# A third block of the masked scores copied by ScalarE instead of multiplied by VectorE, in the feature stage of a four-stage network

## What is computed

```
q = softmax_features(x @ Wq @ Kq)     # softmax of f and of -f, joined: 128 features a head
k = softmax_features(x @ Wk @ Kk)
v = x @ Wv                            # 16 heads of 64
A = causal(q @ k.T)                   # 256 x 256 of a head: zero where the key is later than the query
y = (A @ v) / (sum of A over the keys + 1e-12)
out = y @ Wo
```

## Time and profile before

| | |
|---|---|
| runs of the kernel before | 4855.63 us median of 3 (4854.26 to 4864.38) |
| the profiled execution | 4866.69 us, its span 4865.1 us |
| the feature stage's heads | about 557 to 1280 us of the span |
| busy over 532 to 1280 us (748 us) | PE 706.80, weight loads 584.97, DVE 663.52, ACT 261.51, POOL 456.72 us |
| granted TensorE clock over the same | 0.98 |

### The profile page before, as it was taken

One profiled execution on the slowest core, in us unless ns is written; L12 is line 12 of the kernel. 1 busy time (PEld: TensorE's weight loads), 2 busy tenths in 40 slices (PEclk: granted clock), 3 DMA queues, 4 the chain that ended last, 5 costly groups with the idle time before them and its releaser, 6 DMA issues. The chain is left out here.

```text
span 4865.1 us, 172713 instructions
## 1 busy us (share of the span) xinstructions
PE 4276.7 (88%) x70208; PEld 3382.3 (70%) x70208; DVE 4016.8 (83%) x6281; ACT 3049.4 (63%) x5515; POOL 2776.0 (57%) x1392
## 2 busy tenths in 40 slices
PE   5797799999578999989999999899989999999995
PEld 4565487787557777777777777777777777777774
DVE  5334799999689998989888989989999899898983
ACT  3365333333156777777777777777777777777763
POOL 0222566666266666656666666666666666666661
PEclk9699799999789999999999999999999999999997
DMA  1233000000122324333333233332333323333232
GB/s 49 86 131 123 0 1 0 0 0 0 36 54 62 72 63 93 69 73 68 77 85 70 59 75 81 80 71 63 71 87 77 69 59 75 86 72 74 61 69 56
DMA packets 239188, 303.61 MB, mean 62 GB/s; under 512 B 93940, under 2 KB 129272, under 8 KB 237944
## 3 DMA queue, kind: packets, MB, share of 16 engines
q1 hardware_dynamic: 223192, 247.08, 22.3%
q0 software_dynamic: 15264, 46.14, 3.0%
HBM read 50.37 MB, written 28.84 MB: 16 GB/s over the span
## 5 line engine op out<-in xcount | busy, mean ns | idle before, releaser
L2094 POOL TENSOR_TENSOR raw<-raw,rs 128x1024 f32<-128x1024 f32 x384 | 792.0, 2063 | 985.3 <-DVE rs L1933 628.8
L2086 POOL TENSOR_TENSOR spare<-raw,table 128x1024 f32<-128x1024 f32 x384 | 914.3, 2391 | 261.9 <-DVE raw L1912 251.1
L1905 DVE TENSOR_TENSOR raw<-raw,table 128x1024 f32<-128x1024 f32 x384 | 772.1, 2011 | 55.0 <-POOL spare L2086 53.4
L1779 ACT ACTIVATE raw<-shared 128x512 f32<-128x512 f32 x768 | 463.3, 603 | 309.8 <-PE shared L1559 285.8
L1557 PE MATMUL shared<-wqkv_lo,xT_hi 128*128 128x512 f32 x1152 | 559.8, 486 | 38.9 <-DVE xT_lo L1942 30.1
L1899 DVE TENSOR_REDUCE ss<-spare 128x16 f32<-128x1024 f32 x384 | 466.3, 1215 | 135.2 <-ACT spare L1784 134.6
L1912 DVE TENSOR_TENSOR raw<-raw,spare 128x1024 f32<-128x1024 f32 x384 | 551.0, 1435 | 13.2
L1612 PE MATMUL trn<-ident,raw 128*128 128x128 f32 x3072 | 483.7, 280 | 15.8 <-POOL raw L2094 3.9
L1558 PE MATMUL shared<-wqkv_hi,xT_lo 128*128 128x512 f32 x1152 | 470.4, 408 | 0.0
L1559 PE MATMUL shared<-wqkv_hi,xT_hi 128*128 128x512 f32 x1152 | 469.9, 408 | 0.0
L1784 ACT ACTIVATE spare<-shared 128x512 f32<-128x512 f32 x768 | 462.2, 602 | 1.8 <-DVE ss L1899 1.8
(11 more groups left out here) (203 smaller groups left out, 9740.4 us busy)
## 6 DMA issues: line engine op xcount, KB each, us to landing
Vw<-V SPq DMA_DIRECT2D x1344, 128.0 KB
xs<-X SPq DMA_DIRECT2D x144, 128.0 KB, 2.4
Vw<-V SPq DMA_DIRECT2D x192, 64.0 KB
e_plain<-in_L_ffn_W SPq DMA_DIRECT2D x16, 704.0 KB, 4.7
split_hi<-e_high POOLq DMA_DIRECT2D x16, 704.0 KB, 5.9
split_lo<-e_low POOLq DMA_DIRECT2D x16, 704.0 KB, 7.0
wqkv_hi<-split_hi POOLq DMA_DIRECT2D x30, 256.0 KB, 3.2
wqkv_lo<-split_lo POOLq DMA_DIRECT2D x30, 256.0 KB, 3.3
```

What stands on the lines that cost most here:

```text
L1905: dve.tensor_tensor(x, x, table[:, part, 0, k][:, None, :].to_broadcast([P, H, HD]), ALU.mult).then_inc(cos_part, 1)
L2086: pool.tensor_tensor(dst, src, by[:, None].to_broadcast([P, H, 2, 32]), ALU.mult).then_inc(sin_part, 1)
L2094: pool.tensor_tensor(x, x, rs[:, at:at + H][:, :, None].to_broadcast([P, H, HD]), ALU.mult).then_inc(rotated, 1)
```

## The change

DVE's `mask` multiplies blocks 0 and 2 alone (a view of 2x128 columns with the 128 between them skipped, against one 128-column triangle read twice). ACT gets a new first instruction in every step, `cross(n, h)`, which copies the middle block of head h from PSUM to `at` unchanged. It waits for DVE's `masked` of the same head, so that the two engines don't read the tile at once, and for `mix(h-2)`. A new semaphore `crossed` counts the copies; `scores(h)` and `mix(h)` of PE wait for it beside `masked`.

```
@@ def scores(n, par, h, first):            # PE
                 if not (first and h < 2):
                     pe.wait_ge(masked, count(N - 1))
+                    pe.wait_ge(crossed, count(N - 1))
@@ def mix(n, par, h, first=False):         # PE
                 N = n * H + h
                 pe.wait_ge(masked, count(N + 1))
+                pe.wait_ge(crossed, count(N + 1))
@@ ACT
+            def cross(n, h, first):
+
+                N = n * H + h
+                act.wait_ge(masked, count(N + 1))
+                if not (first and h < 2):
+                    act.wait_ge(mixed, count(N - 1))
+                act.activation(at[:, h % 2, P:SEQ], sco[h % 2][:, P:SEQ], ACT.Copy).then_inc(crossed, 1)
@@ def heads(n, par, first=False, ahead=2): # ACT
                 for h in range(H):
+                    cross(n, h, first)
                     if ahead >= 1:
                         project(n + 1, 1 - par, h)
@@ def mask(n, h, first):                   # DVE
-                dve.tensor_tensor(at[:, h % 2], sco[h % 2][:, 0:3 * P], tri[:], ALU.mult).then_inc(masked, 1)
+                own, to = (x.rearrange("p (c t) -> p c t", t=P)[:, 0:3:2] for x in (sco[h % 2][:, 0:3 * P], at[:, h % 2]))
+                dve.tensor_tensor(to, own, tri[:, None, 0:P].to_broadcast([P, 2, P]), ALU.mult).then_inc(masked, 1)
```

More of the change, by code:

```diff
@@ L761, in feature_stage @@
         masked = sem("g_masked")
+        crossed = sem("g_crossed")
         mixed = sem("g_mixed")
```

## The result

The changed kernel takes 4902.09 us (median of 4 runs, 4898.67 to 4906.06) against 4856.03 for the kernel before on the same chip: ratio 1.0093, 95% interval [1.0079, 1.0106], 46 us slower. The forecast was 4877 with a range to 4894. The sign was right and the size less than half of what came. The profiled execution of the change took 4898.67 us, its span is 4897.1 us.

What follows compares the result with a forecast made beforehand. PE was taken to bound the feature stage, DVE close behind; 1.89 + 0.24 - 0.60 = 1.53 us a sequence over 14 sequences, 21.4 us, gave 4888, or 4877 with medians 11 us lower; range 4848 to 4894.

Steps and rivals of the forecast that it cites:

- What the copy holds up: On ACT, the copy waits for the mask and delays the projection's emptying, so PE waits 1.89 us more a sequence.
- Six places: Projections said to be held at heads 1, 2, 6, 9, 10 and 11, by 0.08 to 0.66 us each.
- The handoff that no row showed: From DVE's mask end to ACT's copy: between 0 and 0.2 us, taken as 0.10.
- The mix of head 13: PE's wait in step 14: the mix needs 0.79 us from its mask's start instead of 0.55, 0.24 more.
- The edge at head 12: ACT's exponential of 1.90 us holds the emptying, which starts 2.46 us after the last; 2.62 are there.
- So the whole wait of 0.60 goes: PE's wait for kept features ahead of step 0's scores vanishes: masks 13 to 15 sooner by 0.39, PE later by 0.24.
- PE's added waits cost nothing where they are met: PE's extra semaphore waits were given no cost, as no idle time showed ahead of turns with three semaphores.
- ACT's emptying isn't held up: Rival: the emptying is done before PE asks; only the two old waits change, -5 us, 4851; chance 0.20 including up to +10.
- DVE's saving in full: Rival: the copy hides, both old PE waits shrink and all 26.9 us go, 4829; chance 0.08, in full or large part.
- The wait on the mask is what carries this term: On ACT, a copy released by the scores alone would hold nothing up and leave the first rival's price, 4851.
- PE's wait for `gen` grows from 1.0 us to about 26: Sign in the changed profile: PE's wait for ACT's emptying of the projection buffer, in five or six places of a sequence.
- The period is about 47.9: Sign in the changed profile: a sequence of the feature stage takes about 47.9 us, where it took 46.40.

Runs made afterwards that it cites:

- copy_behind_drain: The changed kernel with ACT's copy moved behind the emptying of the projection buffer, ahead of the exponential: 4872.78 us, ratio 1.0035 to the kernel before.
- short_mask_no_copy: The kernel before with DVE's mask over blocks 0 and 2 only, the middle block set once to 1.0, no copy: 4856.68 us, ratio 1.0001.
- before_two_more_waits: The kernel before with one always met semaphore wait more on PE at each scores and each mix: 4868.45 us, ratio 1.0027.
- change_one_wait: The changed kernel with PE waiting for `crossed` alone at scores and mix, `masked` dropped: 4888.87 us, ratio 1.0064 to the kernel before.
- full_mask_and_copy: The changed kernel with DVE's mask over all three blocks again and ACT's copy kept: 4921.12 us, ratio 1.0125 to the kernel before.

## Why the prediction was right and wrong

- **What the copy holds up: right.** "So a mask that was needed by the mix, late in step h+1, is now needed before the projection, early in it" is what copy_behind_drain undid. Six places were named, all six came, and no other; 1.89 us a sequence forecast, 2.00 measured. The handoff that no row showed came out shorter (mask end 872.87 to copy 872.91, 0.04 against 0.10), the restart 0.10 longer (1.12 instead of 1.02 for the projection), which the forecast had not counted.
- **The mix of head 13: right.** 0.24 forecast and measured. The edge at head 12 held, and step 13 kept its length.
- **"So the whole wait of 0.60 goes": the first step that failed.** The wait went (-0.64), but it was the cover of another. POOL's operation ended 0.06 us ahead of PE's turn in step 0 in the kernel before, the same 0.06 as with the change, so POOL already set that turn's start. The text looked at waits that show, and this one showed nothing, since the 0.60 of the kept features covered it. 0.40 a sequence, 5.6 us, come back in step 0, so the kept features and step 0 together won 0.24 where the forecast has 0.60; short_mask_no_copy shows it without any copy, and halving POOL's work uncovers the gain.
- **"PE's added waits cost nothing where they are met": right of the place, wrong of the kernel.** This was the largest miss, 9 to 12 us. The argument looked at the turns beside the waits and not at the rest of PE's stream. The term stood at nothing because no idle time showed ahead of PE's turns. before_two_more_waits costs 10 us by the medians, 11.5 in the deep stage, with no other edit; change_one_wait gives 13 back, 9 of them in the deep stage.
- **The clock: not reckoned.** The gap ahead of the mix of head 13 was seen to grow, and only its length was costed. The drops behind it are some 3 us, by the lengths of the sequences that have one.
- The rival "ACT's emptying isn't held up" is refuted for this order of ACT and true for the other (1.0 us of waits in copy_behind_drain). The rival "DVE's saving in full" fails even with the copy left out. "The wait on the mask is what carries this term" was tried with data that need no wait: the period fell to that of before.
- "PE's wait for `gen` grows from 1.0 us to about 26": it shows 10.6. The steps grew by 28 all the same. The sign to watch for was named in a view that counts from a modelled end; the steps' lengths were the right one. "The period is about 47.9" came out as 48.4.

With POOL's 0.40 in the sum, the restarts in the 2.00, 3 for the clock and 11 for the deep stage, the same working gives 28 + 3 + 11 = 42 us of the 46; the rest isn't placed.

## What to carry to other kernels

In an engine's fixed order, ask of every new instruction that waits for another engine what stands behind it and when that is due; here the same copy placed behind one emptying instead of ahead of it was worth 30 us. Behind a wait that is to shrink, look at what the same engine needs next: here POOL's chain ended 0.06 us ahead of PE's next turn, and the 0.40 us won at the waits came back there whole. Let one semaphore stand for two where one is raised behind the other: waits that are always met cost nothing here at their place, and some 10 us elsewhere in the program.

## What the runs showed of the hardware

**PE's instruction stream.** 444 more wait instructions on PE, all met, made an untouched stage 11.5 us longer, 202 more 9 us. The loss is idle time that nothing releases, during bursts in which the DMA engines are 8 to 9 tenths busy. Since half of the waits cost most of the whole, it may be that where in its stream PE stands when a burst begins is what counts; no run shows this, and why the kernels with none more do better wasn't settled.

**The clock after a short gap.** In the changed kernel, in every fourth sequence, the granted clock fell after PE's 1.54 us of waiting at the mix of head 13. The windows view of PE there (busy us, rows, granted clock):

```profile
748.00:749.00 1.00, 0.00 (x0) 1.00 0.00 0
750.00:751.00 1.00, 1.00 (x7) 0.81 0.00 0
751.00:752.00 1.00, 1.00 (x7) 0.50 0.00 0
752.00:753.00 1.00, 1.00 (x7) 0.50 0.00 0
753.00:754.00 1.00, 1.00 (x6) 0.50 0.00 0
754.00:755.00 1.00, 1.00 (x9) 0.98 0.00 0
```

PE goes at 1.2 GHz (0.50) for some 3 us and is back at 2.4 GHz at 754, while it never stopped in between. Four turns (L805) last 1.06 us there instead of 0.60. Step 15 takes 3.7 instead of 2.3 us; POOL's wait in step 0 gives 0.5 of it back, so a drop costs 0.9. In the kernel before, with 1.28 us at this place, the steady part has no drop, nor has change_one_wait with 1.45 us, nor the kernel with the gap filled. With 1.54 us in copy_behind_drain six of 14 sequences have one, and with 1.68 us in full_mask_and_copy eight.

The length of the gap doesn't decide alone. In the reorder of DVE on the kernel before, PE waits 1.2 to 1.3 us ahead of the scores of step 0 in every steady sequence, and in two of them the clock fell as the wait ended, one at 647 us (PE's timeline, then its windows view):

```profile
647.02 1.10 PE L817 MATMUL g_sco<-g_qT,g_kT 128*128 128x256 f32 x2 [1.28 <-DVE g_kT L1012]
```
```profile
646.00:647.00 1.00, 0.00 (x0) 1.00 0.00 0
647.00:648.00 1.00, 0.98 (x3) 0.56 0.00 0
648.00:649.00 1.00, 1.00 (x7) 0.50 0.00 0
```
